# Window attention on TensorE: q times K'V and the next tile's K'V in one stretch, keys and values three tiles ahead, pooled v spread by GpSimd

## What is computed

```python
def _L1_conv_ref(x, qkv_w, proj_w, ...):          # WS=4, DIM=8
    ... # 4x4 windows; xw: (N, C, 4, 4)
    qkv = jnp.einsum('nchw,oc->nohw', xw, qkv_w)
    pooled = _avg_pool5(qkv)
    msq = jnp.concatenate([qkv, pooled], axis=1)
    msq = msq.reshape(N, -1, 3 * DIM, ws * ws).transpose(0, 1, 3, 2)
    q = jax.nn.relu(msq[..., :DIM])
    k = jax.nn.relu(msq[..., DIM:2 * DIM])
    v = msq[..., 2 * DIM:]                          # padded with a column of ones
    kv = jnp.einsum('ngld,nglm->ngdm', k, v)
    out = jnp.einsum('ngld,ngdm->nglm', q, kv)
    out = out[..., :-1] / (out[..., -1:] + 1e-15)
    ... # back to the image
    y = jnp.einsum('nchw,oc->nohw', out, proj_w)
    return y * inv + shift                          # batch norm

x = x + _L0_conv_ref(_gn(x), L0_conv_weight)        # group norm, 3x3 convolution
x = x + _L1_conv_ref(_gn(x), L1_conv_qkv_w, ...)    # group norm, window attention
```

## Time and profile before

| | |
|---|---|
| time, median of 3 runs | 2531.32 us (2529.32 to 2535.28) |
| profiled execution, its own time | 2529.08 us |
| its span | 2527.1 us |
| granted TensorE clock, mean | 0.999 |
| busy: TensorE, weight loads | 98%, 85% |
| busy: VectorE, ScalarE, GpSimd | 68%, 59%, 31% |
| DMA, mean | 23 GB/s |

### The profile page before, as it was taken

One profiled execution on the slowest core, in us unless ns is written; L12 is line 12 of the kernel. 1 busy time (PEld: TensorE's weight loads), 2 busy tenths in 40 slices (PEclk: granted clock), 3 DMA queues, 4 the chain that ended last, 5 costly groups with the idle time before them and its releaser, 6 DMA issues.

```text
span 2527.1 us, 113160 instructions
## 1 busy us (share of the span) xinstructions
PE 2464.9 (98%) x49568; PEld 2156.1 (85%) x49568; DVE 1726.4 (68%) x3609; ACT 1497.3 (59%) x3952; POOL 787.7 (31%) x2164
## 2 busy tenths in 40 slices
PE   4999999999999999999999999999999999999999
PEld 4998889888898888988889888998889978898887
DVE  8876658766587666866668666686666866665665
ACT  2148871488615885168851688427883278823887
POOL 0014430244302443034420444204441044401444
PEclk9999999999999999999999999999999999999999
DMA  4000010000100001000010000100001000000000
GB/s 163 1 2 15 19 59 12 2 18 15 65 6 5 15 18 67 1 5 19 15 67 1 9 15 17 65 1 9 19 15 63 1 13 19 15 9 2 15 19 19
DMA packets 38933, 57.74 MB, mean 23 GB/s; under 512 B 4688, under 2 KB 36304, under 8 KB 36560
## 3 DMA queue, kind: packets, MB, share of 16 engines
q1 hardware_dynamic: 38736, 55.27, 6.2%
HBM read 29.57 MB, written 25.69 MB: 22 GB/s over the span
## 4 chain that ended last, share of the span: by engine, by line
PE 96%; ACT 1%; DVE 1%; issue 1%; DMA 0%; POOL 0%; SPq 0%; POOLq 0%; DVEq 0%
PE ps L319 33%; PE ps L390 16%; PE ps L338 11%; PE ps L365 10%; PE ps L379 9%; PE ps L345 8%; PE ps L354 5%; PE ps L399 3%; ACT ve L568 1%; ACT ve L558 0%; PE ps L304 0%; DMA xs<-w_conv 0%; PE ps L507 0%; DVE st L717 0%; DVE kv_part L867 0%
## 5 line engine op out<-in xcount | busy, mean ns | idle before, releaser
L319 PE MATMUL ps<-dp,wc 128*128 128x392 f32 x4608 | 834.0, 341 | 2.0 <-issue 2.0
L319 PEld LDWEIGHTS ps<-dp,wc 128*128 128x128 f32 x4608 | 816.4, 188 | 3.2 <-issue 2.3
L894 DVE TENSOR_TENSOR kvm<-ps,hm 128x576 f32<-128x576 f32 (+1 forms) x400 | 296.3, 741 | 387.0 <-PE ps L365 386.8
L540 ACT CAST dp<-dt 128x896 fp32r<-128x896 f32 x128 | 120.9, 945 | 558.4 <-PE ps L319 468.0
L1044 POOL TENSOR_TENSOR qm<-qraw 128x64 f32<-128x64 f32 x200 | 61.6, 308 | 1242.8 <-ACT qraw L579 1242.8
L390 PEld LDWEIGHTS ps<-at,wp 128*128 128x128 f32 x3200 | 372.7, 191 | 43.8 <-issue 41.4
L390 PE MATMUL ps<-at,wp 128*128 128x128 f32 (+1 forms) x3200 | 409.2, 281 | 0.4 <-ACT at L603 0.4
L1073 POOL TENSOR_TENSOR xs<-yb,xs 128x128 f32<-128x128 f32 (+3 forms) x560 | 207.3, 397 | 415.4 <-ACT yb L595 415.4
L338 PE MATMUL ps<-wkv,xt 128*128 128x512 f32 x1200 | 331.7, 411 | 0.4 <-ACT ve L568 0.4
L558 ACT ACTIVATE ve<-ps,vmask 128x256 f32<-128x256 f32 x800 | 314.8, 492 | 0.0
L568 ACT ACTIVATE ve<-ps,vmaskp 128x256 f32<-128x256 f32 x800 | 313.4, 484 | 0.0
(11 more groups left out here) (87 smaller groups left out, 2882.7 us busy)
## 6 DMA issues: line engine op xcount, KB each, us to landing
out<-xs SPq DMA_DIRECT2D x224, 112.0 KB, 1.8
xs<-x SPq DMA_DIRECT2D x16, 1344.0 KB, 8.7
xs<-x SPq DMA_DIRECT2D x16, 224.0 KB, 2.7
xs<-w_conv SPq DMA_DIRECT2D x1, 2304.0 KB, 8.5
kvm<-w_kv SPq DMA_DIRECT2D x1, 512.0 KB, 14.4
wp<-w_proj SPq DMA_DIRECT2D x4, 128.0 KB, 8.0
wq<-w_q SPq DMA_DIRECT2D x1, 256.0 KB, 13.9
gav<-gavg SPq DMA_DIRECT2D x1, 64.0 KB, 8.2
```

The lines of the kernel that those rows point to most:

```text
L319: last = nc.tensor.matmul(ps[:, BANK_C[kk % 2][mt], 0:CONV_N], wc[:, part_w, k, kt * TAPS + dy, mt * P:(mt + 1) * P], dp[:, kk % 2, part_d ...
L894: nc.vector.tensor_tensor(kvm[:, h, 0:n].rearrange("p r (g c) -> p r g c", g=2), ps[:, BANK_A + 2 * h:BANK_A + 2 * h + n, 0:2 * PLACES * Q ...
```

## The change

- TensorE's order within a tile becomes: q times K'V of this tile, then both halves of K'V of the next tile (all of them small matmuls, in one stretch), keys and values of the tile after the next two (s+3), q of tile s+2, turning, projection of the tile before (s-1), pooling of tile s+3.
- Keys, values and their pooling run three tiles ahead, so tile 1's are computed within the next image's first convolution chunk (`second_tile`), and tile 2's ahead of the first tile.
- The projection is written behind K'V in banks 4 and 5 (columns from `Y0`), but for the last two tiles, which use bank 0 as before. `yb` is doubled.
- ScalarE copies pooled v once, scaled, into `vpraw`. GpSimd writes it to the four places with one multiplication by `vmask` (`spread_pooled`), `vmaskp` goes.
- The orders of ScalarE, VectorE and GpSimd follow.

The core of the difference (names, semaphores and the convolution's part are cut):

```diff
@@ TensorE, tile(T, e, s)
-                keys_times_values(0, e, units)
-                if not first:
-                    if not final:
-                        pe.wait_ge(xh_low, n2)
-                        pe.wait_ge(y_ready, n0)
-                        q_of_tile(1 - e)
-                    pe.wait_ge(ao_ready, n0)
-                    turn(2)
-                if not final:
-                    pe.wait_ge(vp_ready, n1)
-                    keys_values(n2, 1 - e)
...
-                keys_times_values(1, e, units)
...
-                    project(1 - e, 2)
...
-                attend(e, units)
-                if not final:
-                    pooled(n2)
+                if is_tile(-1):
+                    pe.wait_ge(at_ready, n0)
+                attend(e, units(0))
+                if is_tile(1):
...
+                    keys_times_values(0, 1 - e, units(1))
...
+                    keys_times_values(1, 1 - e, units(1))
+                if is_tile(3):
+                    pe.wait_ge(xh_low, n4)
+                    pe.wait_ge(vp_raw, n3)
+                    keys_values(n4, 1 - e)
+                if is_tile(2):
+                    pe.wait_ge(q_ready, n2)
+                    q_of_tile(e)
+                if is_tile(1):
+                    pe.wait_ge(ao_ready, n1)
+                    turn(units(0))
...
+                    project(1 - e, 2, not is_tile(1))
+                if is_tile(3):
+                    pooled(n4)
@@ ScalarE
             def pooled_keys_values(b, t):
                 act.wait_ge(pool_done, b * TILES + t + 1)
                 nc.scalar.activation(kr[:, t % 2, C:2 * C], ps[0:TT, BANK_KV, 0:C], ACT.Relu, scale=POOL_SCALE)
-                for e in range(PLACES):
-                    last = nc.scalar.activation(
-                        ve[:, t % 2, e, 1].rearrange("p (n m) -> p n m", m=DIM + 1)[:, :, 0:DIM],
-                        ps[0:TT, BANK_KV, C:2 * C].rearrange("p (n m) -> p n m", m=DIM),
-                        ACT.Copy, scale=vmaskp[:, e:e + 1])
-                last.then_inc(vp_ready, 1)
+                if b or t:
+                    act.wait_ge(vp_ready, b * TILES + t)
+                nc.scalar.activation(vpraw[:], ps[0:TT, BANK_KV, C:2 * C], ACT.Copy, scale=POOL_SCALE).then_inc(vp_raw, 1)
...
+                for s in range(-1, TILES):
+                    if s + 3 < TILES:
+                        keys_values(b, s + 3)
+                    if 0 <= s < TILES - 1:
+                        turned(b, s)
                     if s >= 1:
                         batch_norm(b, s - 1)
+                    if s + 4 < TILES:
+                        split_tile(b, s + 4)
+                    if s + 3 < TILES:
+                        pooled_keys_values(b, s + 3)
+                    if s + 2 < TILES:
+                        q_of_tile(b, s + 2)
@@ VectorE
+                for s in range(-1, TILES):
+                    if s >= 0:
+                        weights(b, s)
+                        outputs(b, s)
                     if s + 1 < TILES:
+                        mask(b, s + 1, 0)
+                        mask(b, s + 1, 1)
+                    if s + 4 < TILES:
+                        normalize_tile(b, s + 4)
+                    if s + 1 < TILES:
                         pooled_q(b, s + 1)
+                    if s + 3 < TILES:
+                        kv_low_part(b, s + 3)
+                    if s + 4 < TILES:
+                        tile_low(b, s + 4)
@@ GpSimd
+            def spread_pooled(b, t):
+                pool.wait_ge(vp_raw, b * TILES + t + 1)
+                if b == 0 and t == 0:
+                    pool.wait_ge(set_up, SET_UP)
+                nc.gpsimd.tensor_tensor(
+                    ve[:, t % 2, :, 1].rearrange("p e (n m) -> p e n m", m=DIM + 1)[:, :, :, 0:DIM],
+                    vpraw[:].rearrange("p (n m) -> p n m", m=DIM).unsqueeze(1).to_broadcast([TT, PLACES, C // DIM, DIM]),
+                    vmask[:].unsqueeze(2).unsqueeze(3).to_broadcast([TT, PLACES, C // DIM, DIM]),
+                    ALU.mult).then_inc(vp_ready, 1)
...
+                for s in range(-1, TILES):
+                    if s + 2 < TILES:
+                        pool_q(b, s + 2)
+                    if s + 3 < TILES:
+                        spread_pooled(b, s + 3)
                     if 1 <= s:
                         add_tile(b, s - 1)
@@ around the last image's first tile, and the loop
-WARM_GROUP_NORM, WARM_FIRST_TILE, WARM_START = 4, 16, 22
+WARM_GROUP_NORM, WARM_FIRST_TILE, WARM_TILE, WARM_START = 4, 16, 12, 22
```

More of the change, by code:

```diff
@@ L384, in attend, with project @@
                 last.then_inc(att_done, 1)
[L386 removed]
+            def project(e, units, apart):
                 n = units * TT // 2
                 for mt in range(MT):
+                    y = ps[:, BANK_Q, mt * TT:mt * TT + n] if apart else ps[:, BANK_A + mt, Y0:Y0 + n]
                     for q in range(QUADS):
[L390 to L391 removed]
+                        last = nc.tensor.matmul(y, wp[:, q, mt * P:(mt + 1) * P], at[:, q, e, 0:n],
                                                 start=(q == 0), stop=(q == QUADS - 1))
@@ L403, in tile, with is_tile, units @@
             def tile(T, e, s=None):
[L405 to L410, removed]
-                keys_times_values(0, e, units)
-                if not first:
-                    if not final:
-                        pe.wait_ge(xh_low, n2)
-                        pe.wait_ge(y_ready, n0)
-                        q_of_tile(1 - e)
-                    pe.wait_ge(ao_ready, n0)
-                    turn(2)
-                if not final:
-                    pe.wait_ge(vp_ready, n1)
-                    keys_values(n2, 1 - e)
-                pe.wait_ge(w_loaded, DMA)
-                pe.wait_ge(vp_ready, n1)
-                keys_times_values(1, e, units)
-                if not first:
-                    pe.wait_ge(at_ready, n0)
-                    if not final:
-                        pe.wait_ge(q_ready, n2)
-                    else:
-                        pe.wait_ge(y_ready, n0)
-                    project(1 - e, 2)
+                def is_tile(d):
+                    return s is None or 0 <= s + d < TILES
+                def units(d):
+                    return 2 if s is None else tile_units(s + d)
+                n0, n1, n2, n3, n4 = [held(pe, T + d) for d in range(5)]
+                masks, own_mask = held(pe, T * 2 + 2), held(pe, T * 2 + 3)
                 pe.wait_ge(w_loaded, DMA)
@@ L453, in attention @@
+                pe.wait_ge(w_loaded, DMA)
+                pe.wait_ge(v_ready, t0 + 1)
+                keys_times_values(0, 0, 2)
+                pe.wait_ge(w_loaded, DMA)
+                pe.wait_ge(vp_ready, t0 + 1)
+                keys_times_values(1, 0, 2)
+                pooled(t0 + 3)
+                for s in range(FIRST_LOOPED):
+                    tile(t0 + s, s % 2, s)
                 with pe.Fori(0, LOOPED // 2) as i:
-                    for e in (1, 0):
-                        tile(t0 + i * 2 + (2 - e), e)
@@ L456, in attention @@
-                for s in range(LOOPED + 1, TILES):
+                    for e in range(2):
+                        tile(t0 + FIRST_LOOPED + i * 2 + e, e)
+                for s in range(FIRST_LOOPED + LOOPED, TILES):
                     tile(t0 + s, s % 2, s)
```

98 lines of the change are left out of this document (55 added, 43 removed).

## The result

The changed kernel takes **2749.3 us** (median of 4 runs, 2737.4 to 2756.7); the kernel before, beside it on the same chip, 2530.3 us. The ratio is 1.086, 95% interval [1.081, 1.091]: slower by 219 us, where 2794 us was predicted. The profiled execution took 2756.7 us, its span is 2754.9, 227.8 more than the span before.

What follows compares the result with a forecast made beforehand. TensorE's instruction stream bounds the kernel; with VectorE held during GpSimd's spread, an image's attention grows 32.9 us, times 8 is 263, plus 2 for keep-alive matmuls: 2529 + 263 + 2 = 2794 us, whole range 2500 to 2900.

Steps and rivals of the forecast that it cites:

- its two cases: Whole kernel: VectorE held by the lock for the whole spread, 2794 us; or not held by long instructions, 2473 us.
- TensorE's own work: TensorE's matmul order: two pairs of small/wide changes go, saving 0.70 us per tile (0.46 to 1.20), own period 7.42 us.
- The spread: GpSimd's multiplication of 1024 elements per partition writing pooled v to four places: taken as 2.2 us, between 1.88 and 2.63.
- The wait that comes in: VectorE's normalization and pooled q held by GpSimd's spread, delaying the keys' low part; TensorE idles about 2 us before pooling.
- The period: One looped tile: 9.45 us with VectorE held, 7.68 if nothing else stood in VectorE's way.
- the formula, 7.25 plus the spread: Looped tile's period: 7.25 us plus the length of GpSimd's spread, 9.45 us in all.
- Ends: Attention outside the regular tiles: 7.5 us before the first tile, 8.9 for tile 0, 7.3, 5.3 and 3.0 for tiles 22 to 24.
- Convolution: Keys and pooling of tile 1 move into the convolution: 2.0 us more per image there, hidden by nothing on TensorE.
- Rival 1: VectorE beside the spread: lock does not hold long instructions, or VectorE slips ahead; period 7.68, 2473 us; chance 0.18.
- Rival 2: GpSimd's spread: lock given up between the four places; period 8.75 us, 2670 us; chance 0.04.
- Rival 3: TensorE's clock: idle time in each tile brings stretches at 1.2 GHz, up to 70 us on top; chance 0.06.
- Rival 4: Whole kernel: all effects cancel, within 5 us; chance 0.02.

Runs made afterwards that it cites:

- experiment 1: The changed kernel, but ScalarE writes pooled v to the four places as before the change and GpSimd spreads nothing: 2641.8 us, ratio 1.045 to the kernel before.
- experiment 6: The changed kernel with two orders turned: GpSimd spreads ahead of pooled q, VectorE makes the keys' low part ahead of its pooled-q copies: 2601.4 us, ratio 1.031.
- experiment 3: The kernel of experiment 1, plus a GpSimd multiplication of 1024 elements of constant tiles into a tile nobody reads: 2905.6 us, single run.
- experiment 8: The kernel of experiment 6 with eight more tiles of each image written out instead of looped: 2719.5 us.
- experiment 4: The kernel before, with GpSimd's spread in place of ScalarE's four copies and nothing else: 2539.2 us, ratio 1.0037.

## Why the prediction was right, and where it was not

- **The total.** 2794 us were forecast and 2749 measured, which is nearer than the parts deserve. The forecast's own price of the spread is the difference between its two cases, 2794 and 2473: 321 us. Taking the spread away gave back 107 (experiment 1). The regrouping by itself was to win 56 us (2529 to 2473), and without the spread it loses 115. That these two errors nearly cancel is luck. Right were the direction and the wait that slows the loop.
- **TensorE's own work.** 0.70 us a tile was to be saved. In the loop of experiment 6 TensorE is busy for 128.55 of 130.00 us (540 to 670), and the period is 7.87 and not 7.42. The stretch of small products takes 2.29 us there (577.29 to 579.58), close to the forecast 2.2. The saving is 0.25 us a tile, below even the low end of 0.46: this term was sized too large. A pair of changes between small and wide matmuls costs about 0.12 us by this, an estimate, and not the 0.35 that was read off the weight loader's idle time.
- **The spread.** 1.893 us, at the low end (1.88) of 1.88 to 2.63; the value taken was 2.2. The straight line of packed forms was the right neighbour. Half the size takes 1.040, so 1.67 ns an element and 0.19 us fixed. The estimate of 2.3 us from the Trainium skill, GPSIMD Engine Reference, "3.1 Elementwise — side-by-side cycle accounting", was too high.
- **The wait that comes in.** Right in kind, place and engines: pooling waits for L906, 161 times, and behind the spread VectorE goes in the order described. But it is 1.1 us each time where about 2 was named as the sign, and TensorE is busy for 89% and not 80 to 85: both ends of the gap were misplaced, TensorE's own period (7.42, not about 7.9) and the chain's (9.45, not 8.87). The hold reaches to the end of a 1.89 us instruction (306.84 against 306.92), which the rows before showed for 0.46 only. By the Trainium skill, SBUF — State Buffer, "Who interferes with whom", the lock is held for a full instruction; the trace agrees, now with 1.89 us.
- **The period.** With 1.893 for the spread the formula, 7.25 plus the spread, gives 9.14. But the mean is 8.87. From 308.52 on, with four normalizations ahead of the next pooling, it is 9.15, and from 317.67 on, with two, 8.52. In the loop the spread starts 4.97 us (median) after the start of the pooling before it, where 5.11 was added up, and the next pooling starts 2.02 us after the spread's end, where 2.1 and a handover of 0.06 were taken. These two and the spread's 2.2 make 0.58 us too much a tile, 9.9 us an image over tiles 4 to 20; the spread is the largest of the three.
- **Ends.** Before the first tile 7.5 was forecast, 7.8 came. Tiles 0 to 3 were to take 8.9 + 3 x 9.45 = 37.3 and took 41.5; the last four 9.45 + 7.3 + 5.3 + 3.0 = 25.1 and took 27.2. These 6.3 us an image were not in the sum. TensorE's stops named issue grew from 16.0 to 59.8 us, 5.5 an image, and the lower clock follows many of them: in experiment 6, 16 of the 20 stretches at the lower level begin less than a tile behind a stop of over 1 us. The ends made up for nearly two thirds of what the loop had been given too much.
- **Convolution.** 2.0 us an image more were forecast, and 110.0 against 108.0 are measured.
- **Rival 1**, no lock for long instructions: excluded by the 1249 ns. Its time for a kernel in which nothing is held, 2473 us, was wrong too: experiment 1 has no spread and takes 2642. Its period of 7.68 lies near the 7.87 of experiment 6, but there it is TensorE's own work that sets the period, for which the forecast had 7.42.
- **Rival 2**, the lock given up between the places: excluded by the same row; the hold was one piece.
- **Rival 3**, the clock: in part true. It was granted 0.971 over the span in place of 0.999, and 0.93 in image 1. It does not explain the loop, where it was 0.99 (230 to 370 us). Over the run the lower level stands for 158 us, and TensorE is busy in 137 of them; if all of that work took twice its time it would be 69 us, an estimate and an upper bound. Where TensorE really waited 2.2 us before pooling (experiment 3), the granted clock fell to 0.950, as this rival had it. What it costs by itself was not separated from the stops ahead of it.
- **Rival 4**, all effects cancel: excluded by the 219 us.

What was not asked at all was the question of code. The change moved two tiles more out of the loop and two stretches ahead of it, and the forecast priced their arithmetic and not their being written out. So the 115 us that stay without the spread could not come out of it.

## What to carry to other kernels

When work is handed to GpSimd, write down which VectorE instructions on SBUF fall into its time and whether TensorE has other work until they end: the same 1.9 us multiplication cost 9 us in one order and 107 in another, and turning two orders, GpSimd's and VectorE's, around it won back 148 us, more than the 107 of taking it away. When a pipeline is made deeper, count the tiles that leave the loop; here each one written out cost 0.8 to 1.8 us beyond its arithmetic, and the packets of the instruction queue in the page tell how many there are. A loop that is 0.25 us a tile faster is then easily lost at its ends.

## What the runs showed of the hardware that was not expected

- Written-out code of small matmuls makes TensorE stop for 1 to 2.6 us at a time. It goes on in the median 2.4 us after a 16 KB instruction packet has started; a packet more cost 0.42 us in the old order of work and 1.03 in the merged one, and nothing of this is seen while a loop goes round.
- Behind such a stop the granted clock can fall to the 1.2 GHz level for a few us: in experiment 8 it is 0.50 from 647.99 to 650.10, behind the stop of 2.23, and 63 K'V products took 2.17 us, where experiment 6, undisturbed, has 64 in 1.23.
- A GpSimd multiplication whose product nobody reads cost 264 us on top of 2642, 205 of them as TensorE's wait for VectorE, and one of half the length in its proper place cost nothing (one run each).
- VectorE's mask, which reads PSUM, kept its 0.75 us inside a spread (experiment 4), while its normalizations on SBUF were held.
